# A four-stage transformer pipeline on one core: the wait for the rows of ones moved, and the last three layer norms shared with ScalarE

## The chip, the core and the metric

The kernel runs on one core of a Trainium2 chip. The core has a matrix engine (TensorE, PE in the profile, with its weight loads as PEld), a vector engine (VectorE, DVE), an engine for activation functions (ScalarE, ACT), a general engine (GpSimd, POOL) and a queue engine that issues the DMAs here (SyncE, SP). They run their own instruction streams and meet at semaphores. The metric is the device time of one execution in microseconds (us).

## The reference, cut to what matters

Input x has 8 batches of 512 tokens with 128 features. Four stages follow each other, each closed by a residual and a layer norm:

```python
x = layernorm(x + attention0(x))   # softmax attention, 16 heads of 8 features
x = layernorm(x + experts(x))      # 32 routed experts of width 64 (6 chosen per token), one shared of width 128
x = layernorm(x + attention1(x))   # RMS-normed q and k, rotary, sigmoid weights divided by their sum
x = layernorm(x + ffn(x))          # width 384: (silu(x Wg) * (x Wu)) Wd, weights int32 / 127
```

The layer norm of a row of 128 features is `(x - mean) / sqrt(var + 1e-5)`. The change touches the start of the first stage and the end of the last one.

## The kernel before, in words

**First attention.** q and k are split in three bf16 parts each; for each head the pairs of parts stand as 48 rows of a stack (`qs`, `ks`), two heads to a tile, one at partition 0 and one at 64. A first pass of scores (`s1`, L564) uses these 48 rows, and VectorE takes the maximum of every row of scores (`reduce_max`, L724). GpSimd splits the negated maxima in three parts (`split_max`, L788 to L794), TensorE turns them (`turn_max`, L542), ScalarE copies them out, and a DMA puts them under `qs` as rows 48 to 50. The second pass (`s2`, L629) multiplies 51 rows: rows 48 to 50 of `ks` are ones, so that the maximum is subtracted inside the product, and ScalarE takes the exponential (L483). The ones come from DRAM by DMA (`ones_rows`, L393, from `in_fill`), four of them, which raise `fill_in` to 64.

**The start.** Batch 0 takes a quicker way than the others. Its q and k products land in PSUM (L681), ScalarE and VectorE split them (L508 to L766), and for the first four heads (two stack tiles, `PLACED = 2`) TensorE puts the parts in place with products against a selection matrix (L695), which are copied to `qs` and `ks` (L516, L771; `placed`). The other heads go through DRAM: the SP queue writes the parts (L234, L240) and reads the stacks back (L253). Behind these reads stand, on the same queue, the ones for batch 0 (L393), the load of the residual X for all batches (L435), and the writes of batch 1's parts. Dummy products (`warm_up`, L533) stand between. GpSimd's first work on tensors is to split q and k of batch 1 (`split_qk`, L263 to L271); its stream waits for the load of X first (`pool.wait_ge(x_in, 16)`, ahead of `walk`). In the lead, which handles batch 0 alone, TensorE walks a fixed list of turns, two per unit: 56 scores, one V product, q and k of batch 1 (L554), and after the 39th score `turn_max` of the first half of the heads. Then `s2` begins. All orders here are written out by hand; there is no scheduler.

**The end.** The last stage (`last_stage`) has three hidden slices per batch, 24 units. Per unit TensorE makes gate and up products (L2220 to L2222), ScalarE silu (L2279), VectorE the product `hid` (L2309), ScalarE its rounded part `hh` (L2285), GpSimd the rest `hl` (L2352; VectorE for the last, L2335), and three units later TensorE adds the down products (L2244 to L2250). At the end of a batch ScalarE takes the sums (`take_down`, L2291), TensorE turns them (`turn`, L2257), VectorE adds X (L2318) and takes mean and variance (L149, L153), GpSimd makes `rstd` with an addition and a power (L183, L185), VectorE scales (L162, for the last batch L2326), and SP writes the batch out (L2209, and the last batch in two halves, L2213). Batches alternate between two banks (`out_bank`: 6 and 7), so a batch's first down product waits until the batch two before it has been scaled (`x_done`).

## Time and profile before

| | us |
|---|---|
| median of 3 runs | 1071.41 (1071.37 to 1071.44) |
| the profiled execution, its own time | 1071.79 |
| span of the profile | 1070.0 |
| PE busy | 1004.1 (94%) |
| DVE busy | 807.5 (75%) |
| ACT busy | 737.0 (69%) |
| POOL busy | 475.0 (44%) |

The span runs from the first instruction to the last event; the device time is 1.79 us longer in the profiled execution. Times in rows count from the start of the span. A row of the timeline merges equal instructions that follow each other; the duration is the time in which at least one of them was busy. Matmuls overlap: one of 512 columns is shown with 0.39 us, and the next can start 0.22 us after it at the full clock. PE counts as busy with dummy products too, so its 94% do not say that it is the limit.

### The profile page before, as it was taken

To read this page: it belongs to the slowest core of one execution; us is meant where nothing else is said; L and a number is where in the kernel's file an instruction comes from. 1 tells how busy PE (TensorE), PEld (TensorE's weight loads), DVE (VectorE), ACT (ScalarE), POOL (GpSimd) and SP (SyncE) were. 2 spreads that over 40 slices of the span, in tenths; PEclk is the share of its full clock that TensorE was granted. 3 is DMA by queue.
4 is the path that set the end of the run, shared out by engine and by line. 5 is a ranking of instruction groups with operands and counts; after the bars stand their busy time and mean duration, and the time that the engine had idled before them with its cause. 6 is when DMAs were issued, how large, how long until landed. Compare 5 with 4: busy or idle time off the path is not lost. (4 is left out here: it accounts for less than half of the span.)

```text
span 1070.0 us, 20246 instructions
## 1 busy us (share of the span) xinstructions
PE 1004.1 (94%) x5869; PEld 479.0 (45%) x5869; DVE 807.5 (75%) x1864; ACT 737.0 (69%) x955; POOL 475.0 (44%) x485
## 2 busy tenths in 40 slices
PE   4999999999999998999999999988999999999996
PEld 2322222222222235888888887762232323222485
DVE  3899999999999975897788789956456545632477
ACT  2047877777777786655555555557988898899754
POOL 0313414235143725676677677565332333220175
PEclk7999999999999999999999999999999999999999
DMA  6264122231221003234333432442512331230011
GB/s 194 93 223 125 46 86 75 70 114 45 86 81 52 2 2 115 93 114 149 113 93 123 140 111 80 145 145 68 161 63 65 118 112 58 65 118 1 1 31 50
DMA packets 73981, 96.98 MB, mean 91 GB/s; under 512 B 12668, under 2 KB 42236, under 8 KB 73532
## 3 DMA queue, kind: packets, MB, share of 16 engines
q1 hardware_dynamic: 73928, 96.33, 28.8%
q8 instruction: 26, 0.43, 0.2%
q14 instruction: 27, 0.22, 0.1%
HBM read 68.11 MB, written 27.79 MB: 90 GB/s over the span
## 5 line engine op out<-in xcount | busy, mean ns | idle before, releaser
L724 DVE TENSOR_REDUCE a_nmax<-a_ps_f 128x1 f32<-128x512 f32 x512 | 320.1, 683 | 28.2 <-PE a_ps_f L564 27.6
L483 ACT ACTIVATE a_prob<-a_ps_s 128x1024 f32<-128x1024 f32 x256 | 251.7, 1022 | 76.2 <-PE a_ps_s L629 74.9
L1314 ACT ACTIVATE a_prob<-a_ps_s 128x1024 f32<-128x1024 f32 x256 | 244.8, 1030 | 35.7 <-PE a_ps_s L1368 34.8
L2141 POOL TENSOR_TENSOR moe_hl<-moe_hid,moe_hh 128x512 fp32r<-128x512 f32 x135 | 175.2, 1303 | 90.1 <-ACT moe_hh L2026 90.0
L564 PE MATMUL a_ps_f<-a_ks,a_qs 48*128 48x512 bf16 x512 | 157.9, 387 | 22.2 <-DMA a_ks<-in_fill 10.7
L2016 ACT ACTIVATE moe_ps<-moe_ps 128x512 f32<-128x512 f32 x128 | 74.5, 582 | 112.0 <-PE moe_ps L1943 111.4
L1381 PE MATMUL a_ps_o<-a_prob,a_va 128*32 128x512 f32 x1024 | 137.3, 608 | 1.0 <-ACT a_prob L1314 0.5
L642 PE MATMUL a_ps_o<-a_prob,a_va 128*32 128x512 f32 x1024 | 136.4, 605 | 0.5 <-ACT a_prob L483 0.4
L629 PE MATMUL a_ps_s<-a_qs,a_ks 51*128 51x512 bf16 x512 | 132.5, 381 | 1.7 <-ACT a_prob L483 1.5
L564 PEld LDWEIGHTS a_ps_f<-a_ks,a_qs 48*128 48x128 bf16 x512 | 39.8, 93 | 202.6 <-DVE a_nmax L724 161.3
L2067 DVE TENSOR_TENSOR moe_prod<-moe_cw,moe_ps 128x512 f32<-128x512 f32 x128 | 87.3, 682 | 29.7 <-PE moe_ps L1943 29.1
L1368 PE MATMUL a_ps_s<-a_qs,a_ks 48*128 48x512 bf16 x512 | 92.7, 387 | 12.7 <-ACT a_prob L1314 9.4
L2076 DVE TENSOR_TENSOR moe_hid<-moe_prod,moe_ps 128x512 f32<-128x512 f32 x128 | 86.9, 679 | 6.6 <-DVE moe_prod L2067 1.9
L2026 ACT ACTIVATE moe_hh<-moe_hid 128x512 fp32r<-128x512 f32 x136 | 84.7, 624 | 3.7 <-DVE moe_hid L2076 3.6
L263 POOL TENSOR_TENSOR a_parts<-a_qk,g_zero 128x512 bf16<-128x512 f32 x28 | 29.2, 1044 | 126.1 <-ACT a_qk L455 65.7
L1368 PEld LDWEIGHTS a_ps_s<-a_qs,a_ks 48*128 48x128 bf16 x512 | 23.6, 93 | 134.2 <-ACT a_prob L1314 107.2
L788 POOL TENSOR_TENSOR a_msplit<-a_nmax,g_zero 128x32 bf16<-128x32 f32 x16 | 3.8, 239 | 145.6 <-DVE a_nmax L724 145.6
L1941 PE MATMUL moe_ps<-moe_xh,moe_whig 128*128 (+1 forms) x136 | 54.8, 403 | 2.0 <-DVE moe_hid L2076 2.0
L1966 PE MATMUL moe_ps<-moe_hl,moe_whid 128*128 128x512 f32 x136 | 53.9, 396 | 1.5 <-POOL moe_hl L2141 1.5
L1941 PE MATMUL moe_ps<-moe_xh,moe_whiu 128*128 (+1 forms) x136 | 53.8, 395 | 0.0
L1942 PE MATMUL moe_ps<-moe_xh,moe_wlog 128*128 (+1 forms) x136 | 53.7, 395 | 0.0
L1961 PE MATMUL moe_ps<-moe_hh,moe_wlod 128*128 128x512 f32 x136 | 53.7, 395 | 0.0
(304 smaller groups left out, 1630.6 us busy)
## 6 DMA issues: line engine op xcount, KB each, us to landing
moe_cw<-r_weights SPq DMA_DIRECT2D x256, 128.0 KB, 2.9
parts_q<-a_parts SPq DMA_DIRECT2D x48, 256.0 KB, 2.5
parts_k<-a_parts SPq DMA_DIRECT2D x48, 256.0 KB, 2.5
a_qs<-parts_q SPq DMA_DIRECT2D x126, 96.0 KB, 2.4
a_ks<-parts_k SPq DMA_DIRECT2D x126, 96.0 KB, 2.4
a_xt<-in_x_t SPq DMA_DIRECT2D x8, 256.0 KB, 3.0
out_x<-g_X SPq DMA_DIRECT2D x7, 256.0 KB, 2.3
moe_wg<-in_wg SPq DMA_DIRECT2D x1, 1088.0 KB, 6.7
```

The source lines that it names most:

```text
L483: nc.scalar.activation(prob[:, u % PSLOTS, :, :], ps_s[:, u % 2, :, :], ACT.Exp, scale=float(P) ** -0.5).then_inc(exp_done, 1)
L564: nc.tensor.matmul(ps_f[:, bank, :], stack_rows(qs[p], h, QKR)[:, qt * P:(qt + 1) * P], stack_rows(ks[p], h, QKR), start=True, stop=True). ...
L629: mm = nc.tensor.matmul(ps_s[:, u % 2, i, :], stack_rows(ks[p], h, MXR)[:, kt * P:(kt + 1) * P], stack_rows(qs[p], h, MXR), start=True, st ...
L642: mm = nc.tensor.matmul(ps_o[j * CT:(j + 1) * CT, :], v_of_head(va[p], kt, grp * HG + j), prob[:, (2 * e + j // UN) % PSLOTS, j % UN, :], ...
L724: nc.vector.tensor_reduce(nmax[:, half_no, h % 2, col:col + 1], ps_f[:, bank, :], AX.X, ALU.max, negate=True).then_inc(max_done, 1)
L1314: nc.scalar.activation(prob[:, u % PSLOTS, :, :], ps_s[:, u % 2, :, :], ACT.Sigmoid, scale=float(HD) ** -0.5).then_inc(exp_done, 1)
L1368: mm = nc.tensor.matmul(ps_s[:, u % 2, i, :], stack_rows(ks[p], h, QKR)[:, kt * P:(kt + 1) * P], stack_rows(qs[p], h, QKR), start=True, st ...
L1381: mm = nc.tensor.matmul(ps_o[j * CT:(j + 1) * CT, :], v_of_head(va[p], kt, grp * HG + j), prob[:, (2 * e + j // UN) % PSLOTS, j % UN, :], ...
L1941: nc.tensor.matmul(dst, w[0][:, j, :], hi, start=True, stop=False)
L2067: nc.vector.tensor_tensor(prod[:, bank(j), :], cw[:, slot(j), :], ps_u[:, bank(j), :], ALU.mult).then_inc(prod_done, 1)
L2076: nc.vector.tensor_tensor(hid[:, hid_at(j), :], prod[:, bank(j), :], ps_g[:, bank(j), :], ALU.mult).then_inc(hid_done, 1)
L2141: nc.gpsimd.tensor_tensor(hl[:, part_at(j), :], hid[:, hid_at(j), :], hh[:, part_at(j), :], ALU.subtract).then_inc(hl_done, 1)
```

## The change

At the start, the wait for the rows of ones (`fill_in`) stands ahead of the first `s2` of batch 0 instead of ahead of the whole walk. The selection products go tile by tile (both q and k of tile 0, then of tile 1), and their readers wait for other counts. The dummy products ahead of them are two instead of four. At the end, batches 5, 6 and the second half of 7 are scaled on ScalarE as `rstd * y + shift`, where `shift = -mean * rstd` comes from VectorE; batch 5's `rstd` still comes from GpSimd, those of 6 and 7 from a ScalarE root and a VectorE reciprocal. Batch 7's down sums go to bank 0 (a gate bank that is free then) and their transposes to the first halves of banks 0 and 1, so its first down product no longer waits for batch 5's scaling.

```diff
-WARM = (5, 4, 3)
+WARM = (5, 2, 3)
...
-                act.wait_ge(first_done, 4 + (1, 2, 4)[k])
+                act.wait_ge(first_done, 4 + (1, 3, 4)[k])
...
+                if is_first(b) and u == 0:
+                    pe.wait_ge(fill_in, 4 * 16)
                 if u in (0, NU // 2):
...
-            for n in range(2):
-                pe.wait_ge(first_mid, 2 * n + 2)
-                pe.wait_ge(first_low, 2 * n + 2)
-                for j in range(PLACED):
+            for j in range(PLACED):
+                for n in range(2):
+                    if j == 0:
+                        pe.wait_ge(first_mid, 2 * n + 2)
+                        pe.wait_ge(first_low, 2 * n + 2)
...
             pe.wait_ge(cleared, 5)
-            pe.wait_ge(fill_in, 4 * 16)
             walk(pe, units)
...
-            dve.wait_ge(first_done, 4 + 3)
+            dve.wait_ge(first_done, 4 + 2)
...
         def out_bank(b):
-            return ps[:, 6 + b % 2, :]
+            return ps[:, 6 + b % 2, :] if b < NB - 1 else ps[:, (N - NH3) % RG, :]
+
+        def tiles(b):
+            if b < NB - 1:
+                return out_bank(b).rearrange("p (k d) -> p k d", k=NT)
+            return ps[:, 0:2, 0:T // 2].rearrange("p n (k d) -> p n k d", k=NT // 2)
...
-            for i in range(2):
-                sp.wait_ge(ln["x_done"], NB + i)
+            for i, (done, value) in enumerate(((x_last, 1), (ln["x_done"], NB))):
+                sp.wait_ge(done, value)
...
-                elif j == 0 and b >= 2:
+                elif j == 0 and 2 <= b < NB - 1:
                     pe.wait_ge(ln["x_done"], b - 1)
...
+            def deviation(b):
+                n = LATE_B.index(b)
+                st, at = stats_of(b)
+                act.wait_ge(st["dve"], 2 * NT * (at + 1))
+                nc.scalar.activation(rs[:, n, :], st["mv"][:, :, 1], ACT.Sqrt,
+                                     bias=g["eps"][:, 0:1]).then_inc(std_done, 1)
+
+            def apply(b, which):
+                n = LATE_B.index(b)
+                act.wait_ge(shift_done, n + 1)
+                for k in which:
+                    y = tiles(b)[:, k, :] if b < NB - 1 else tiles(b)[:, k // 2, k % 2, :]
+                    ins = nc.scalar.activation(X[:, b, k, :], y, ACT.Identity, scale=scale_of(b)[:, k:k + 1],
+                                               bias=shift[:, n, k:k + 1])
+                ins.then_inc(ln["x_done"], 1)
...
+                if s == N:
+                    nc.scalar.activation(last.table[:, :], g["zero"][:, :], ACT.Sqrt)
+            apply(LATE_B[0], range(NT))
+            deviation(LATE_B[1])
+            apply(LATE_B[1], range(NT))
+            deviation(LATE_B[2])
+            apply(LATE_B[2], range(NT // 2, NT))
...
+                if b == NB - 1:
+                    scale(NB - 2)
                 dve.wait_ge(y_done, b + 1)
...
+            def scale(b):
+                n = LATE_B.index(b)
+                dve.wait_ge(std_done, n)
+                nc.vector.reciprocal(rs[:, n, :], rs[:, n, :]).then_inc(rs_done, 1)
+                dve.wait_ge(rs_done, n)
+                shifts(b)
...
             def apply_last():
                 b = NB - 1
-                dve.wait_ge(ln_last["pool"], 2)
-                for k in range(NT):
-                    ins = nc.vector.tensor_scalar(X[:, b, k, :], tiles(b)[:, k, :], ln_last["mv"][:, k, 0:1],
-                                                  ln_last["rstd"][:, k:k + 1], ALU.subtract, ALU.mult)
-                    if k % 2:
-                        ins.then_inc(ln["x_done"], 1)
+                for k in range(NT // 2):
+                    ins = nc.vector.tensor_scalar(X[:, b, k, :], tiles(b)[:, 0, k, :], ln_last["mv"][:, k, 0:1],
+                                                  rs[:, 2, k:k + 1], ALU.subtract, ALU.mult)
+                ins.then_inc(x_last, 1)
...
                 if s == N:
+                    dve.wait_ge(ln["pool"], 2 * (NB - 3) + 2)
+                    shifts(NB - 3)
                     dve.wait_ge(hh_done, N)
...
-                if batch_at(s, Y_AT) is not None:
-                    b = batch_at(s, Y_AT)
-                    layernorm_pool(nc, pool, g, *((ln, b) if b < NB - 1 else (ln_last, 0)))
+                if batch_at(s, Y_AT) is not None and batch_at(s, Y_AT) < NB - 2:
+                    layernorm_pool(nc, pool, g, ln, batch_at(s, Y_AT))
```

The order in which TensorE works at the start, before the change (`a_ps_s<-a_parts,a_prob` is a selection product, `a_ps_f<-a_ks,a_qs` a score of the first pass, `x5` counts equal rows):

```order
L695 MATMUL a_ps_s<-a_parts,a_prob 112x512 [waits a0_first_mid,a0_first_low,a0_first_rest,a0_select_in]
L695 MATMUL a_ps_s<-a_parts,a_prob 112x512 x5
L695 MATMUL a_ps_s<-a_parts,a_prob 112x512 [waits a0_first_low,a0_first_mid]
L695 MATMUL a_ps_s<-a_parts,a_prob 112x512 x5
L564 MATMUL a_ps_f<-a_ks_88,a_qs_87 128x512 [waits a0_placed0,a0_fill_in,a0_stack_in0,a0_cleared,consts_in]
```

And the same place in the changed kernel:

```order
L699 MATMUL a_ps_s<-a_parts,a_prob 112x512 [waits a0_first_mid,a0_first_low,a0_first_rest,a0_select_in]
L699 MATMUL a_ps_s<-a_parts,a_prob 112x512 x2
L699 MATMUL a_ps_s<-a_parts,a_prob 112x512 [waits a0_first_low,a0_first_mid]
L699 MATMUL a_ps_s<-a_parts,a_prob 112x512 x8
L565 MATMUL a_ps_f<-a_ks_88,a_qs_87 128x512 [waits a0_placed0,a0_stack_in0,a0_cleared,consts_in]
```

The score no longer waits for `a0_fill_in`, and the second half of the parts is needed three products earlier. The wait now stands on the first 51-row product (L632), behind 56 scores of the same stream.

ScalarE's stream at the very end, in the changed kernel (before it ended with the second `ff_dsb` row here, without the table load between):

```order
L2312 ACTIVATE ff_dsb<-ff_ps 128x512 [waits ff_t_done,ff_d_done]
L2306 ACTIVATE ff_hh<-ff_hid 128x512 [waits ff_d_done,ff_hid_done]
L2339 ACT_TABLE_LOAD
L2339 ACTIVATE a_table<-g_zero 128x1
L2312 ACTIVATE ff_dsb<-ff_ps 128x512 [waits ff_t_done,ff_d_done]
L2326 ACTIVATE g_X<-ff_ps,ff_shift,ff_rstd 128x128 [waits ff_shift_done]
L2326 ACTIVATE g_X<-ff_ps,ff_shift,ff_rstd 128x128 x3
L2318 ACTIVATE ff_rs<-ff_mv,g_eps 128x4 [waits ff_ln_dve]
L2326 ACTIVATE g_X<-ff_ps,ff_shift,ff_rs 128x128 [waits ff_shift_done]
L2326 ACTIVATE g_X<-ff_ps,ff_shift,ff_rs 128x128 x3
L2318 ACTIVATE ff_rs<-last_mv,g_eps 128x4 [waits last_ln_dve]
```

Behind these rows stand the two halves of batch 7 (`L2326`). Four scalings of batch 6 now stand between two roots on one engine. VectorE's stream at the end of the changed kernel:

```order
L2359 TENSOR_TENSOR ff_ps<-ff_ps,g_X 128x2x256 [waits ff_t_done]
L2368 RECIPROCAL ff_rs<-ff_rs 128x4 [waits ff_std_done]
L2374 SCALAR_TENSOR_TENSOR ff_shift<-ff_mv,ff_rs 128x4 [waits ff_rs_done]
L150 BN_STATS last_st<-ff_ps 128x6 [waits ff_y_done]
L150 BN_STATS last_st<-ff_ps 128x6 x3
L152 MEMSET last_gate 128x1 [waits last_ln_dve]
L154 BN_AGGR last_mv<-last_st 128x2 x4
L2368 RECIPROCAL ff_rs<-ff_rs 128x4 [waits ff_std_done]
L2374 SCALAR_TENSOR_TENSOR ff_shift<-last_mv,ff_rs 128x4 [waits ff_rs_done]
L2380 TENSOR_SCALAR g_X<-ff_ps,last_mv,ff_rs 128x128 x2
```

Before, four scalings of batch 6 stood behind `last_mv` and ahead of four of batch 7 (`g_X<-ff_ps,...`), and four of batch 5 stood between the last two `ff_hid`. Now VectorE scales two tiles in all here, and between the last addition and its statistics stands a reciprocal that waits for ScalarE's root.

## Rows read from the trace of the kernel before

**Rows 1.** Windows: stretch, length, PE, PEld, DVE, ACT, POOL busy, clock share, DMA share, GB/s
```profile
62.40:168.00 105.60, 101.41 (x658) 27.62 (x658) 100.46 (x184) 82.06 (x93) 35.48 (x49) 1.00 0.34 111
```
**Rows 2.** Timeline to 40 us: start, busy, engine, line, operation, count, idle before and releaser
```profile
9.99 2.77 PE L695 MATMUL a_ps_s<-a_parts,a_prob 128*112 128x512 bf16 x12 [0.31 <-issue]
...
20.58 0.88 SPq L435 DMA_DIRECT2D g_X<-in_x  x1
...
23.42 0.61 PE L564 MATMUL a_ps_f<-a_ks,a_qs 48*128 48x512 bf16 x2 [10.66 <-DMA a_ks<-in_fill]
...
29.11 0.39 PE L564 MATMUL a_ps_f<-a_ks,a_qs 48*128 48x512 bf16 x2
...
38.02 1.04 POOL L263 TENSOR_TENSOR a_parts<-a_qk,g_zero 128x512 bf16<-128x512 f32 x1 [37.11 <-ACT a_qk L455]
```
**Rows 3.** The load of X (L435), from issue to landing
```profile
DMA to landing us min/median/max: 11.1/11.1/11.1
```
**Rows 4.** Timeline of 40 to 63 us
```profile
41.48 1.15 POOL L271 TENSOR_TENSOR a_parts<-a_rest,a_parts 128x512 bf16<-128x512 f32 x1
...
43.90 1.04 POOL L263 TENSOR_TENSOR a_parts<-a_qk,g_zero 128x512 bf16<-128x512 f32 x1 [1.27 <-ACT a_qk L455]
...
49.44 0.24 POOL L794 TENSOR_TENSOR a_msplit<-a_mrest,a_msplit 128x32 bf16<-128x32 f32 x1
...
51.79 0.26 PE L542 MATMUL a_ps_f<-a_identb,a_msplit 128*96 128x128 bf16 x1 [0.21 <-DVE a_nmax L724]
...
58.88 0.51 PE L564 MATMUL a_ps_f<-a_ks,a_qs 48*128 48x512 bf16 x2
...
60.08 0.51 PE L564 MATMUL a_ps_f<-a_ks,a_qs 48*128 48x512 bf16 x2
...
62.47 0.39 PE L629 MATMUL a_ps_s<-a_qs,a_ks 51*128 51x512 bf16 x2
```
**Rows 5.** Windows of 1 us, columns as in rows 1
```profile
15.00:16.00 1.00, 0.00 (x0) 0.00 (x0) 0.00 (x0) 0.00 (x0) 0.00 (x0) 0.59 0.13 41
28.00:29.00 1.00, 1.00 (x3) 0.21 (x3) 0.97 (x2) 0.00 (x0) 0.00 (x0) 0.58 1.06 293
745.00:746.00 1.00, 1.00 (x8) 0.46 (x9) 0.96 (x4) 0.00 (x0) 0.00 (x0) 0.82 0.98 345
749.00:750.00 1.00, 1.00 (x10) 0.11 (x5) 0.00 (x0) 1.00 (x2) 0.00 (x0) 0.98 0.82 209
```
**Rows 6.** PE's timeline of 713 to 750 us, two idle stretches
```profile
719.25 0.61 PE L1368 MATMUL a_ps_s<-a_qs,a_ks 48*128 48x512 bf16 x4 [1.73 <-ACTq L1319]
...
744.93 0.66 PE L1351 MATMUL a_ps_f<-g_ident,a_xr 128*128 128x128 f32 x4 [1.51 <-DVE a_xr L1470]
```
**Rows 7.** Timeline of the last 14 us
```profile
1058.77 0.47 PE L2244 MATMUL ff_ps<-ff_hh,ff_whid 128*128 128x512 f32 x1 [0.36 <-DVE g_X L162]
...
1059.25 0.63 ACT L2285 ACTIVATE ff_hh<-ff_hid 128x512 fp32r<-128x512 f32 x1 [0.20 <-DVE ff_hid L2309]
...
1061.59 0.60 ACT L2291 ACTIVATE ff_dsb<-ff_ps 128x512 f32<-128x512 f32 x1 [1.71 <-PE ff_ps L2250]
...
1062.93 0.70 DVE L2318 TENSOR_TENSOR ff_ps<-ff_ps,g_X 128x512 f32<-128x512 f32 x1 [0.38 <-PE ff_ps L2257]
...
1064.69 0.28 DVE L153 BATCH_NORM_AGGREGATE last_mv<-last_st 128x2 f32<-128x6 f32 x3
...
1066.37 1.37 DVE L2326 TENSOR_SCALAR g_X<-ff_ps,last_mv,last_rstd 128x128 f32<-128x128 f32 x4
1067.13 1.01 SPq L2213 DMA_DIRECT2D out_x<-g_X  x2
```
**Rows 8.** ScalarE's timeline around a table load in the second stage
```profile
437.47 1.28 ACT L998 ACT_TABLE_LOAD   x1
438.76 0.28 ACT L998 ACTIVATE moe_exp<-moe_ps 128x128 f32<-128x128 f32 x1
```
**Rows 9.** Groups by form: line to count, then busy us, mean ns, idle before
```profile
L1795 DVE RECIPROCAL r_den<-r_den 128x4 f32<-128x4 f32 x8 | 1.4, 177 | 0.3
```

More of the change, by code:

```diff
@@ L142, in layernorm_buffers @@
             "rstd": sb("rstd", [P, NT]), "gate": sb("gate", [P, 1]),
-            "dve": sem("ln_dve"), "pool": sem("ln_pool"), "centred": sem("ln_centred"), "x_done": sem("x_done")}
+            **{k: sem(k if k == "x_done" else "ln_" + k) for k in signals}}
 def layernorm_stats(nc, dve, ln, b, y):
     for k in range(NT):
-        nc.vector.bn_stats(ln["st"][:, k, :], y[:, k, :]).then_inc(ln["dve"], 1)
+        tile = y[:, k, :] if len(y.shape) == 3 else y[:, k // 2, k % 2, :]
+        nc.vector.bn_stats(ln["st"][:, k, :], tile).then_inc(ln["dve"], 1)
     dve.wait_ge(ln["dve"], 2 * NT * b + NT)
@@ L2189, in last_stage, with scale_of, stats_of @@
                              "t_done", "y_done"))
-        last_lo, ln_last = sem("last_lo"), layernorm_buffers(ctx, nc, "last")
+        last_lo, ln_last = sem("last_lo"), layernorm_buffers(ctx, nc, "last", ("dve",))
+        LATE_B = (NB - 3, NB - 2, NB - 1)
+        rs, shift = sb("rs", [P, 3, NT]), sb("shift", [P, 3, NT])
+        std_done, rs_done, shift_done, x_last = sem("std_done"), sem("rs_done"), sem("shift_done"), sem("x_last")
         def out_bank(b):
-            return ps[:, 6 + b % 2, :]
+            return ps[:, 6 + b % 2, :] if b < NB - 1 else ps[:, (N - NH3) % RG, :]
[3 more added lines that the diff above has]
+            return ps[:, 0:2, 0:T // 2].rearrange("p n (k d) -> p n k d", k=NT // 2)
+        def scale_of(b):
+            return ln["rstd"] if b == LATE_B[0] else rs[:, LATE_B.index(b), :]
+        def stats_of(b):
+            return (ln, b) if b < NB - 1 else (ln_last, 0)
         def batch_at(s, at):
@@ L2256, in turn @@
                 for q in range(NT):
-                    mm = nc.tensor.transpose(out_bank(b)[:, q * P:(q + 1) * P], dsb[:, q * P:(q + 1) * P],
+                    to = tiles(b)[:, q, :] if b < NB - 1 else tiles(b)[:, q // 2, q % 2, :]
+                    mm = nc.tensor.transpose(to, dsb[:, q * P:(q + 1) * P],
                                              g["ident"][:, :])
@@ L2338, in _ @@
                     add_x(batch_at(s, Y_AT))
-                if batch_at(s, Y_AT) == NB - 1:
-                    layernorm_apply(nc, dve, g, ln, NB - 2, tiles(NB - 2))
-                elif batch_at(s, APPLY_AT) is not None and batch_at(s, APPLY_AT) < NB - 2:
+                if batch_at(s, APPLY_AT) is not None and batch_at(s, APPLY_AT) < NB - 3:
                     layernorm_apply(nc, dve, g, ln, batch_at(s, APPLY_AT), tiles(batch_at(s, APPLY_AT)))
                 elif batch_at(s, APPLY_AT) == NB - 1:
+                    scale(NB - 1)
                     apply_last()
```

17 lines of the change are left out of this document (10 added, 7 removed).

## The prediction

> **What bounds the kernel now.** I read the windows by stage, then the timeline of the start and of the end, then the clock. In the first attention's steady stretch VectorE is busy 100.46 of 105.60 us [rows 1]: it is the pace there, and a start that comes earlier should be kept as long as VectorE's first maximum comes earlier. It comes late: TensorE ends the selection products at 9.99 + 2.77 = 12.76 us, then stands idle 10.66 us until 23.42, released by the DMA that writes the ones [rows 2]. No first-pass score reads these rows. At the end nothing overlaps any more: after the last down product come ScalarE's copy (61.59), the transposes, VectorE's addition (62.93), statistics that end at 64.69 + 0.28 = 64.97, GpSimd's root until 66.37, four scalings in 1.37 us, and the last write [rows 7]. The reader is to see two separate gains, each with something that could come to stand in its place.
>
> **The wait for the ones.** Without it the first score waits only for its stacks, whose copies follow the selection products, and for these products themselves on TensorE. Their order by tile brings the first pair of copies earlier, but the second half of the parts is needed earlier too, and TensorE still has twelve of them to do: the first score starts at about 12.9. The reorder and the two dummy products fewer I cost at nothing (from −0.3 to +0.3 us): TensorE works on until 12.76 either way. So scores start 23.42 − 12.9 = 10.5 us earlier.
>
> The clock adds to it. The granted clock fell to half (1.2 instead of 2.4 GHz) at about 15.2 us, in that idle stretch (the mean share of 0.59 in that microsecond means 18% of it at full), and came back at about 28.8 [rows 5]. Meanwhile three pairs of scores took from 23.42 to 29.11, 5.69 us [rows 2]; at the full clock a pair takes 60.08 − 58.88 = 1.20 us [rows 4], three take 3.6. Without the idle stretch 2.1 us more are saved. TensorE would be at `turn_max` (L542), which stood at 51.79 [rows 4], at 51.79 − 10.5 − 2.1 = 39.2.
>
> But this instruction waits for GpSimd, and GpSimd's stream does not move with the scores. Its first split waits for the load of X, which stands on SP's queue behind the same transfers as before: issued at 20.58, landed 11.1 us later, at 31.7 [rows 2, 3]. Before, it was hidden: GpSimd started at 38.02, when ScalarE had q [rows 2]. Now q is there some 12.6 us earlier, at about 25.3, and X is last. From 31.85 (0.15 us from release to start) the split of q takes 41.48 + 1.15 − 38.02 = 4.61 us, and k and the split of the maxima 49.44 + 0.24 − 43.90 = 5.78 us [rows 2, 4]; the pause of 1.27 us between them goes, since k is there by then. GpSimd ends at 31.85 + 4.61 + 5.78 = 42.25 and `turn_max` starts at 42.4, 9.4 us earlier than before, not 12.6. From it to the first 51-row product (62.47) [rows 4] is 10.7 us of scores in VectorE's pace, as before; pairs of 1.20 us are its pace already, so nothing is caught up. Behind `turn_max` in TensorE's stream wait the last 16 scores, and VectorE for those. The moved wait itself costs nothing: the ones land by 23.4 and are asked for at 53.
>
> TensorE is idle from 39.2 to 42.4, 3.2 us. Does the clock fall? It fell about 2.4 us into the idle stretch at the start, and just after one of 1.51 us that ended at 744.93, but not for one of 1.73 us that ended at 719.25 [rows 5, 6]. I take that it falls. It then stays low for about 749.04 − 745.64 = 3.4 us (shares 0.82 and 0.98) [rows 5], or at worst the 5.4 us from 23.42 to 28.8. Of each low microsecond 1 − 1.20 / 1.90 = 0.37 is lost, so 1.3 us, at worst 2.0. The start brings 9.4 − 1.3 = 8.1 us; ends 7.2 and 9.7.
>
> The rest of the three attention and expert stages keeps its order. One thing moves with time: the low clock at 745.6 to 749.0 followed an idle stretch no longer than one that left the clock alone [rows 5, 6], so such falls can appear or vanish. Each is worth at most 3.4 × 0.37 = 1.3 us. I take zero and keep ±1.3.
>
> **The end.** The first down product of batch 7 waited 0.36 us for batch 5's scaling [rows 7]; this goes. Batch 5's four scalings leave VectorE ahead of its last hidden product, and the 0.20 us that ScalarE waited for it go too [rows 7]. I take 0.4 us for ScalarE's copy: 61.19 instead of 61.59. What is late next is the new table load, on ScalarE between the last `hh` (which would end at 59.25 − 0.20 + 0.63 = 59.68) and this copy. Loads took 1.28 us, with 0.02 us on either side [rows 8], and the small root behind it at most the 0.28 us of a 128x128 activation: 61.2, just covered; another 0.1 to 0.2 us would show.
>
> The Trainium skill (ScalarE: Activation LUTs, What ACT_TABLE_LOAD costs) says that every switch costs the load and a drain, about 2.66 us together. In rows 8 the next activation starts right behind the load, so this trace does not bear the drain out; by the rule the copy would start at about 62.5.
>
> Then ScalarE scales. This trace has no activation with a scale and a bias per partition. From below stands the 128x128 activation with 0.28 us [rows 8], four of them at most 1.1 us, and 0.8 us if they overlap by 0.1 us each (an estimate); from above the one of 512 columns with 0.60 us [rows 7], four 2.4 us. Nearest in kind is VectorE's scaling of the same tiles with the same two operands, four in 1.37 us [rows 7], and I take that.
>
> By the same page and section each such operand adds about 93 ns; an estimate from its figures is 1.6 us for four, which would leave about 0.6 us of the gain at the end instead of 0.9.
>
> Laid out: copy 61.19, VectorE's addition 62.53 to 63.23. ScalarE scales batch 5 from 61.7 to 63.1 and takes the root for batch 6 to 63.3. VectorE's reciprocal (0.18 us [rows 9]) waits for it and, with `shift`, lets the statistics of batch 7 start at 63.6, about as before: the 0.4 us is spent. They end at 64.9. ScalarE is scaling batch 6 from 63.75 to 65.12, so the root of batch 7 comes at 65.12 and ends at 65.35; reciprocal and `shift` until 65.7; VectorE scales two tiles until 66.43, ScalarE the other two until 66.54. GpSimd's way took from 64.97 to 66.37; the new one takes until 65.7, and half of the scalings are beside it. The last write is issued at about 66.9 (the first of the two holds the queue) instead of 67.74, the end of the four scalings [rows 7]. Gain 0.9 us. With 0.8 us for four it is 1.2; with 2.4 us the statistics start at 64.6, the root of batch 7 at 67.2, and it is a loss of 1.2 us.
>
> **The sum.** 8.1 + 0.9 = 9.0 us. The profiled execution took 1071.79 us, its span 1070.0 and 1.79 outside it; it would become 1062.8. It was 0.38 us above the median of 1071.41, against which the forecast is 1062.4.
>
> **The rivals.**
>
> *The clock holds.* If TensorE's idle stretch at `turn_max` does not lower the clock, as at 719.25, the start brings 9.4 us: 1071.41 − 10.3 = 1061.1. For it: the stretch could be cut if TensorE arrives later. Against: 3.2 us is longer than the 2.4 us after which it fell. A vanished fall at 745 would give a similar time.
>
> *GpSimd does not hold it.* Were X there before q, `turn_max` would move by the whole 12.6 us: 1071.41 − 12.6 − 0.9 = 1057.9. For it speaks only that a landing time is of one execution; the queue ahead of X is unchanged.
>
> *The gain at the start is given back.* If something not seen pins the first exponentials or the loop (such as the loads behind the stacks), only the end is left: 1070.5. Against: in the steady stretch VectorE idles 5 us in 106 [rows 1], and all else moves along.
>
> *Slower: the clock stays low through the lead.* With fewer dummy products and scores of only 48 rows, TensorE could be left at 1.2 GHz from its first scores. A pair then takes 1.90 us instead of 1.20, the 28 pairs 53 us, and the first 51-row product starts at 12.9 + 53 = 66 plus V, q and k (about 2 us), 68 instead of 62.47: 1071.4 + 5.6 − 0.9 = 1076. It decides from (9.4 + 0.9) / 0.70 = 15 pairs at the low clock on. Against: from 28.8 us on the same mix of scores and dummies ran at the full clock [rows 5].
>
> *The end is lost, by the drain.* If the switch of tables took twice what rows 8 show, the copy and all behind it would come 1.3 us later, for a loss of 0.4 us at the end: 1071.41 − 8.1 + 0.4 = 1063.7. For it speaks nothing in the trace; against it, that the activation at 438.76 follows the load at once [rows 8]. It is the case of the skill's drain, named above.
>
> **How the numbers follow.** Forecast (clock falls once, end near +0.9) 0.48; the drain 0.04; the clock holds, or a fall elsewhere vanishes, 0.32; GpSimd does not hold it 0.04; given back 0.06; slower 0.06. Likeliest time 1062.4. The range reaches down to the clock that holds with one fall less, 1061.1 − 1.3 = 1059.8, and up to the price of 2.0 us for the fall with an end worth nothing, 1071.41 − 7.4 = 1064.0, rounded to 1064.3. A measurement of this kernel can tell 0.2%, 2.1 us. Faster: the first four of these cases and half of the given-back one (its 1070.5 lies within 0.2%, but it may be given back in part), 0.91; within 0.2%: 0.03; slower 0.06.
>
> **What would show it.** In the new profile: first score at 12.9 (later would be the copies); GpSimd's first split at 31.8, not at q; an idle stretch of TensorE ahead of `turn_max` released by GpSimd's last split, near 42.4; clock share of 0.5 for about 3.4 us behind it; first exponential near 54.8; at the end ScalarE's last copy no longer idle for long before it, no `rstd` on GpSimd for batches 6 and 7, the root of batch 7 released by ScalarE's own scalings rather than by the statistics. I am wrong if the first split starts elsewhere, if the steady loop takes longer than before, or if the time from ScalarE's last copy of sums to the end of the span (1070.0 − 61.59 − 1000 = 8.4 us before) does not fall to about 7.9.

## The result and the profile after

The changed kernel took 1065.78 us (median of four executions, 1064.63 to 1067.31); the kernel before, beside it, 1071.43 us (1071.37 to 1073.59). The ratio is 0.9935, with a 95% interval from 0.9908 to 0.9962. The forecast was 1062.4 us with a range up to 1064.3: the direction was right, the time was not. Of a forecast gain of 9.0 us the profile shows 4.5 (span 1070.0 before, 1065.5 after); it is of the slowest of the four executions (1067.31), and by the medians 5.65 us were gained and 3.4 are missing. One execution of the kernel before in a later comparison took 4970.9 us and is left out of every figure.

At the start each row came where it was forecast. The timeline of the changed kernel to 55 us (columns as in rows 2):

```profile
9.81 3.08 PE L699 MATMUL a_ps_s<-a_parts,a_prob 128*112 128x512 bf16 x12 [0.76 <-DVE a_rest L765]
12.82 0.39 PE L565 MATMUL a_ps_f<-a_ks,a_qs 48*128 48x512 bf16 x2
...
31.69 1.04 POOL L264 TENSOR_TENSOR a_parts<-a_qk,g_zero 128x512 bf16<-128x512 f32 x1 [30.78 <-DMA g_X<-in_x]
...
41.80 0.24 POOL L797 TENSOR_TENSOR a_msplit<-a_mrest,a_msplit 128x32 bf16<-128x32 f32 x1
...
42.19 0.24 PE L543 MATMUL a_ps_f<-a_identb,a_msplit 128*96 128x128 bf16 x1 [2.80 <-POOL a_msplit L797]
...
54.65 1.02 ACT L484 ACTIVATE a_prob<-a_ps_s 128x1024 f32<-128x1024 f32 x1 [11.84 <-PE a_ps_s L632]
```

The first score starts at 12.82 us (12.9 forecast; 23.42 in [rows 2]). GpSimd's first split is released by the load of X at 31.69 (31.85 forecast; 38.02 in [rows 2], where ScalarE released it). TensorE waits 2.80 us for GpSimd's last split and is at `turn_max` at 42.19 (42.4 forecast; 51.79 in [rows 4]). The first exponential comes at 54.65, 8.25 us earlier than before.

The reader is to look for the rest in the clock column. Windows of the changed kernel, columns as in rows 1 (the ninth number of a row, ahead of the DMA share, is the clock share; 0.50 is 1.2 GHz):

```profile
42.30:45.60 3.30, 3.30 (x9) 0.77 (x9) 1.35 (x3) 0.27 (x1) 0.00 (x0) 0.50 0.59 197
...
406.00:407.00 1.00, 0.00 (x0) 0.00 (x0) 0.00 (x0) 0.49 (x1) 0.00 (x0) 1.00 0.60 191
407.50:410.90 3.40, 3.40 (x10) 2.87 (x11) 0.85 (x3) 2.07 (x3) 1.28 (x1) 0.50 0.60 166
411.00:412.00 1.00, 1.00 (x6) 0.81 (x5) 0.87 (x3) 0.16 (x1) 0.00 (x0) 1.00 0.85 207
...
670.40:673.70 3.30, 3.30 (x9) 2.61 (x8) 1.69 (x4) 1.63 (x3) 1.28 (x1) 0.50 0.21 75
...
714.70:718.10 3.40, 3.40 (x20) 2.06 (x20) 1.49 (x8) 2.40 (x3) 3.04 (x8) 0.50 0.57 177
...
742.00:745.40 3.40, 3.40 (x18) 0.48 (x20) 1.29 (x3) 1.88 (x2) 0.00 (x0) 0.50 0.52 161
```

The first of these was forecast, and the last answers to that of 745.6 to 749.0 in [rows 5]. The three between them are new. TensorE's timeline shows an idle stretch of more than a microsecond ahead of each (the number in brackets is the idle time). Those at 407 and 714 us stand at boundaries of stages, directly behind it. The one at 670 us stands inside the experts, 1.4 us behind the transposes of X for the second attention, which followed an idle stretch of 1.63 us:

```profile
407.50 1.09 PE L974 MATMUL moe_ps<-g_ident,moe_dsb 128*128 128x128 f32 x4 [1.74 <-PEq L296]
...
668.24 0.66 PE L1113 MATMUL moe_ps<-g_ident,g_X 128*128 128x128 f32 x4 [1.63 <-DVE a_turned L1080]
...
714.33 0.72 PE L1371 MATMUL a_ps_s<-a_qs,a_ks 48*128 48x512 bf16 x4 [1.72 <-ACTq L1322]
...
741.04 0.66 PE L1354 MATMUL a_ps_f<-g_ident,a_xr 128*128 128x128 f32 x4 [1.53 <-DVE a_xr L1473]
```

The third row is the stretch of [rows 6] that was 1.73 us long and left the clock alone in the kernel before.

To see what each costs, the same instruction was looked up in both traces, and its start before subtracted from its start after. This shift is −8.24 us up to the end of the first attention and changes only at the low stretches: to −6.6 behind 407 us, from −6.5 to −4.9 behind 670 us, to −3.9 behind 715 us, and not behind 742 us, since the kernel before has its own low stretch there. It is −3.80 us at the last stage. The steady stretch keeps its pace (VectorE busy 100.9 of 106.0 us in its window from 54 to 160 us, 100.46 of 105.60 in [rows 1]).

The end, in the timeline of the changed kernel (add 3.8 us to compare with rows 7):

```profile
1055.14 0.62 ACT L2306 ACTIVATE ff_hh<-ff_hid 128x512 fp32r<-128x512 f32 x1
...
1055.78 1.28 ACT L2339 ACT_TABLE_LOAD   x1
...
1057.08 0.20 ACT L2339 ACTIVATE a_table<-g_zero 128x1 f32<-128x1 f32 x1
...
1057.39 0.60 ACT L2312 ACTIVATE ff_dsb<-ff_ps 128x512 f32<-128x512 f32 x1
1057.88 1.50 ACT L2326 ACTIVATE g_X<-ff_ps,ff_shift,ff_rstd 128x128 f32<-128x128 f32 x4
...
1060.91 0.28 DVE L154 BATCH_NORM_AGGREGATE last_mv<-last_st 128x2 f32<-128x6 f32 x3
1061.39 0.30 ACT L2318 ACTIVATE ff_rs<-last_mv,g_eps 128x4 f32<-128x4 f32 x1
1061.73 0.18 DVE L2368 RECIPROCAL ff_rs<-ff_rs 128x4 f32<-128x4 f32 x1 [0.53 <-ACT ff_rs L2318]
...
1062.14 0.81 ACT L2326 ACTIVATE g_X<-ff_ps,ff_shift,ff_rs 128x128 f32<-128x128 f32 x2 [0.44 <-DVE ff_shift L2374]
...
1062.77 0.89 SPq L2233 DMA_DIRECT2D out_x<-g_X  x2
```

On the old scale (less 1000) ScalarE's copy comes at 1057.39 + 3.80 − 1000 = 61.19, as forecast; the statistics of batch 7 end at 1061.19 + 3.80 − 1000 = 64.99 (64.9 forecast), its root starts at 65.19 (65.12 forecast), and the last scalings end at 1062.95 + 3.80 − 1000 = 66.75 (66.54 forecast). The end brings 0.7 us instead of 0.9: 0.4 ahead of ScalarE's copy, as forecast, and 0.3 behind it. From that copy to the end of the span are 1065.5 − 1057.4 = 8.1 us, where the prediction named 7.9 as its sign.

### The profile page after: what moved, and what is told of

Read it like the earlier page. It is cut to its first block and busy times, and to the rows that moved or that the text cites. A ratio compares the mean times of both kernels' runs of the same rounds, so it can differ in the third digit from the quotient of the medians.

```text
span 1065.5 us, 20246 instructions
## 1 busy us (share of the span) xinstructions
PE 1008.0 (95%) x5867; PEld 481.8 (45%) x5867; DVE 805.6 (76%) x1859; ACT 742.8 (70%) x969; POOL 472.6 (44%) x481
## 5 line engine op out<-in xcount | busy, mean ns | idle before, releaser
L632 PE MATMUL a_ps_s<-a_qs,a_ks 51*128 51x512 bf16 x512 | 132.6, 381 | 1.7 <-ACT a_prob L484 1.5
L1371 PE MATMUL a_ps_s<-a_qs,a_ks 48*128 48x512 bf16 x512 | 92.9, 389 | 12.3 <-ACT a_prob L1317 9.0
```

The costliest lines, as they stand in the source:

```text
L632: mm = nc.tensor.matmul(ps_s[:, u % 2, i, :], stack_rows(ks[p], h, MXR)[:, kt * P:(kt + 1) * P], stack_rows(qs[p], h, MXR), start=True, st ...
L1371: mm = nc.tensor.matmul(ps_s[:, u % 2, i, :], stack_rows(ks[p], h, QKR)[:, kt * P:(kt + 1) * P], stack_rows(qs[p], h, QKR), start=True, st ...
```

## The experiments

Three readings of the 4.4 us that the profile lost between the start and the last stage were open. **A**: granted-clock falls at idle stretches of TensorE that may or may not fall in an execution. **B**: the new end or the new order of the selection products costs it. **C**: transfers or barriers at the boundaries give back part of any gain. Below, "shift" is always against the first profile of the kernel before. Each ratio is against the executions of the kernel before on the same chip beside it.

**Only the wait is moved.** The kernel before, with this edit alone:

```diff
             def s2(b, p, u):
+                if is_first(b) and u == 0:
+                    pe.wait_ge(fill_in, 4 * 16)
...
-            pe.wait_ge(fill_in, 4 * 16)
             walk(pe, units)
```

> The kernel before with one edit: the wait for the ones stands ahead of the first sums of probabilities (s2) instead of ahead of all scores. Order of the selection products, dummy products and the whole end are as before. Theory A (clock): the first exponential is 8.0 to 9.0 us earlier than before (GpSimd's split still starts at about 31.7 us), and this shift is kept on VectorE and ScalarE except where a low stretch of the clock stands in one kernel and not in the other; each such stretch takes 1.0 to 1.7 us of it. With two to four more stretches than before the time is 1071.4 - 8.3 + (2 to 5) = 1065 to 1068; the shift changes at low stretches and nowhere else. Theory B (the gain is lost in the new end or in the new order of the selection products): with neither of them in, the time is 1071.4 - 8.3 = 1063.1. Theory C (a fixed share of the gain is lost at the boundaries of stages, to transfers that do not come earlier): the shift shrinks at the two boundaries by more than the low stretches there explain, and TensorE waits there for a DMA.

Measured: 1065.94 us beside 1073.21 of the kernel before, ratio 0.9931 (0.9908 to 0.9955), which is the changed kernel's. The shift in its profile is −7.09 us at the first exponential, outside the 8 to 9 expected: the low stretch at `turn_max` was twice as long (41.9 to 48.6), and another stood at the start of the loop:

```profile
41.90:48.60 6.70, 6.51 (x17) 1.42 (x17) 3.27 (x5) 0.27 (x1) 0.05 (x1) 0.50 0.66 197
58.90:65.70 6.80, 6.45 (x28) 1.03 (x29) 3.97 (x7) 2.91 (x4) 3.24 (x5) 0.50 0.56 194
```

The second took 2.4 us of the shift, to −4.69, more than the 1.0 to 1.7 us expected of each. It is a place that the prediction did not think of. B falls for the start: with neither new order nor new end, the last stage comes 4.5 us earlier and not 8.3.

**Only the end is new.** The changed kernel with its start put back (the order of the selection products, too):

```diff
-WARM = (5, 2, 3)
+WARM = (5, 4, 3)
...
-                if is_first(b) and u == 0:
-                    pe.wait_ge(fill_in, 4 * 16)
...
+            pe.wait_ge(fill_in, 4 * 16)
             walk(pe, units)
```

> The changed kernel with its start (dummy products, order of the selection products, place of the wait for the ones) put back as before; only the end is new. Theory A: up to the last stage the instructions start when they did in the kernel before, to 0.2 us, the low stretches of the clock are those of before (one at about 15 to 29 us, one at about 746 to 749 us), and the time is 0.7 us less, 1070.7 (1070.2 to 1071.2). Theory B (the end costs what is missing): 1071.4 + 3 or more. The table load stands alone in 1.3 us and the next activation follows it at once; four scalings take 1.5 us.

Measured: 1071.48 us, ratio 0.9982 (0.9965 to 0.9999). In its profile the shift goes from +0.21 us at the last stage's hidden products to −0.41 where the last `rstd` is ready and −0.46 at the end of the span, so the end gives 0.7 us there; the ratio allows that and more. The time lies above the 1070.2 to 1071.2 expected. B falls for the end too. That it would start as the first profile of the kernel before, with the same low stretches, was wrong: the first stretch was 10.2 us long instead of 13.7, so that the first exponential came 1.5 us earlier, and it had one at 675 and one of 6.8 us at 719 us, and none at 746.

**GpSimd waits for X where it first reads it.** In the changed kernel:

```diff
                 if u0 == 0 and is_first(b):
+                    pool.wait_ge(x_in, 16)
                     front.split_weight(pool, 0)
...
-            pool.wait_ge(x_in, 16)
...
```

> The changed kernel with GpSimd's wait for X put where GpSimd first reads X (the first unit of batch 0) instead of ahead of its first split. Theory A: GpSimd's first split starts when ScalarE has q, at about 25.5 us instead of 31.7, the first maximum's transpose (turn_max) is no longer waited for by TensorE and comes at 39.2 to 39.8 us instead of 42.2, the low stretch of 3.4 us behind it is gone, and the first exponential comes 12 to 12.6 us earlier than in the kernel before (4 us earlier than in the changed one). The end follows, minus low stretches at the boundaries (0 to 3 of them at 1.0 to 1.7 us): 1071.4 - 12.3 - 0.7 = 1058.4 with none, up to 1063 with three. Rival (something behind the split holds the first maximum as well, such as VectorE's or GpSimd's later work on X): turn_max stays at about 42 and the time at 1065.8.

Measured: 1059.83 us (1058.54 to 1063.51), ratio 0.9876 (0.9849 to 0.9903). Its timeline, and two of its windows:

```profile
25.79 1.04 POOL L264 TENSOR_TENSOR a_parts<-a_qk,g_zero 128x512 bf16<-128x512 f32 x1 [24.87 <-ACT a_qk L456]
...
39.55 0.26 PE L543 MATMUL a_ps_f<-a_identb,a_msplit 128*96 128x128 bf16 x1 [0.21 <-DVE a_nmax L727]
...
50.66 1.95 ACT L484 ACTIVATE a_prob<-a_ps_s 128x1024 f32<-128x1024 f32 x2 [10.48 <-PE a_ps_s L632]
```

```profile
30.00:50.00 20.00, 19.74 (x82) 6.20 (x80) 18.63 (x32) 0.87 (x2) 5.71 (x9) 1.00 0.50 156
...
404.00:407.30 3.30, 3.30 (x10) 2.65 (x9) 1.30 (x4) 1.60 (x3) 1.28 (x1) 0.50 0.59 170
```

The split starts at q, `turn_max` is no longer held, the clock stays at 1.00, and the first exponential comes 12.24 us earlier than before. So the wait for X held the start, as the prediction said, and it cost 4.0 us against the changed kernel's first profile: 2.6 at `turn_max` (39.55 for 42.19), and 1.35 for the low stretch behind it. The shift stays at −12.23 until the one fall at 404 us, which takes 1.59.

**TensorE kept busy in the wait.** The changed kernel, with dummy products where it waits for GpSimd:

```diff
+HOLD = 12
...
+                        if is_first(b):
+                            warm_up(HOLD)
                         turn_max(b, 0)
```

> The changed kernel with twelve dummy products on TensorE directly ahead of the first maximum's transpose, where it otherwise waits 2.8 us for GpSimd. They take about 2.6 us at the full clock. Theory A: the clock stays high there, the transpose comes at the same 42.2 us, and the first exponential comes 1.2 us earlier than in the changed kernel (53.4 instead of 54.65). What the end of the program keeps of it depends on the low stretches at the boundaries: 1064.5 if they are the same as in the changed kernel, and 1.0 to 1.7 us more or less for each that comes or goes. Rival (the low stretch at 42.3 us does not come from the wait ahead of it): it stands there as before, and the time is unchanged or 0.1 us more.

Measured: 1066.05 us, ratio 0.9918 (0.9893 to 0.9942). The dummies did what they were for, and it brought nothing in this profile:

```profile
38.00:55.00 17.00, 16.55 (x73) 5.50 (x72) 13.98 (x24) 2.10 (x3) 3.28 (x7) 1.00 0.66 215
56.10:66.30 10.20, 9.85 (x42) 1.61 (x41) 6.62 (x11) 5.14 (x6) 4.74 (x5) 0.50 0.69 255
```

The first exponential came 9.73 us earlier, but a low stretch of 10.2 us at the start of the loop took 3.5 us of it (shift −6.20 behind it). That the fall is gone behind `turn_max` is shown; why another came at 56 us is not. TensorE had idled no longer than 0.21 us at a time from 38 us on. This is one profile.

**Both kernels again, twice.** The same two programs, unchanged.

> The changed kernel once more, unchanged. Theory A (which idle stretches lower the clock differs between executions of one program): the start and the steady stretches are as in the first profile to 0.2 us (turn_max at 42.2 us), but the low stretches behind the boundaries at 407, 670, 715 and 742 us are not all the same ones or not of the same length; the times spread over 2 us or more, and those with a lower mean granted clock are longer by about 0.4 us for each low microsecond. Rival (the four falls belong to the program): the same four stretches stand there, and the times agree to 0.5 us.

Measured: 1064.75 us (1063.95 to 1065.41), ratio 0.9923 (0.9906 to 0.994). Its profile has low stretches at 41 (6.8 us), 669 and 713 us and none at 407 or 742, so the falls differ between executions of one program, as expected. The other two parts were not borne out: the times spread over 1.5 us and not over 2 or more, and they do not follow the mean granted clock (1064.55 us at 0.989, 1065.41 at 0.991).

> The kernel before once more, unchanged. Theory A: at the boundaries (about 412, 675, 720 us) low stretches can stand that its first profile does not have, which gives times up to 6 us above the fastest; its median is above the 1071.4 of its first three runs. Rival: one fall at 746 us as in the first profile, and 1071.4 to 0.3 us.

Measured: 1072.01 us (1070.61 to 1073.29), ratio 0.9991 (0.998 to 1.0002). The median is above 1071.4, as expected. Three windows of its profile, two where the first profile has the clock at full and one where it has it low:

```profile
65.00:71.80 6.80, 6.45 (x27) 0.95 (x29) 3.90 (x7) 2.92 (x4) 3.32 (x5) 0.50 0.86 329
...
720.40:727.10 6.70, 6.26 (x26) 2.73 (x27) 3.82 (x14) 3.88 (x4) 4.17 (x9) 0.50 0.29 92
745.00:750.00 5.00, 3.48 (x28) 1.32 (x24) 2.77 (x7) 3.10 (x4) 2.09 (x2) 1.00 0.46 157
```

The fall at 746 us is not there, and two others are.

> The changed kernel, one more profiled execution. Theory A: turn_max at 42.2 us and a low stretch behind it; low stretches at some of the places seen so far (about 56, 407, 670, 714, 742 us) and at no others, not the same set as in both earlier profiles. Rival: the set of its first profile.

Measured: one execution, 1064.13 us. Its low stretches are at 43, 668 and 712 us; in its window from 404 to 408 us, over the first boundary, the clock share is 1.00.

> The kernel before, one more profiled execution. Theory A: one low stretch from about 15 to 17 us until 26 to 29 us, then a set out of about 65, 412, 675, 720 and 746 us; the end is later than the fastest execution by about 0.4 us for each low microsecond. Rival: one fall at 746 us alone, as in the first profile.

Measured: one execution, 1072.53 us, with low stretches at 16, 675 and 746 us.

**The boundaries filled.** In the changed kernel:

```diff
             pv(NB - 1, 1, NE - 1)
+            columns = identb[:, :].unsqueeze(1).broadcast_to([P, NT, P])
+            for _ in range(5):
+                nc.tensor.matmul(ps_s[:, 0, 0, :], identb[:, :], columns, start=True, stop=True)
...
+            def fill(b, count):
+                if routed and isinstance(b, int) and b == NB - 1:
+                    for _ in range(count):
+                        nc.tensor.matmul(ps_g[:, 0, 0:P], g["ident"][:, :], g["ident"][:, :], start=True, stop=True)
...
             def turn(b):
+                fill(b, 4)
                 pe.wait_ge(d_taken, b + 1 + C)
...
                 mm.then_inc(t_done, 1)
+                fill(b, 8)
```

> The changed kernel with dummy products on TensorE in three idle stretches at the boundaries: five behind the last product of the first attention (the idle stretch of 1.7 us ahead of the experts' first transposes), four and eight small ones around the last transposes of the experts (0.7 and 1.7 us). The idle stretch of 1.6 us ahead of the transposes of X for the second attention is left as it is. Theory A: no low stretch behind 407 and 715 us any more, that at 670 us may stand; the first exponential stays at 54.6 us, and the end keeps 1.6 to 3.5 us more of the gain than the first profile did: 1063.3 (1062 to 1065). Rival (the 4.4 us lost on the way are not the clock's): the time stays at 1065.8 or grows by the dummy products' 1 to 2 us, with the shift shrinking at the same places.

Measured: 1064.44 us (1063.62 to 1066.14), ratio 0.9921 (0.9902 to 0.994), the changed kernel's in its second comparison. Windows of its profile:

```profile
403.00:409.00 6.00, 4.58 (x30) 1.70 (x31) 0.28 (x1) 4.46 (x6) 0.00 (x0) 1.00 0.38 131
669.00:672.40 3.40, 3.40 (x10) 2.63 (x9) 1.90 (x5) 1.64 (x4) 1.28 (x1) 0.50 0.25 81
705.00:716.00 11.00, 9.37 (x59) 7.16 (x58) 3.47 (x13) 5.43 (x9) 5.58 (x7) 1.00 0.12 37
```

As expected, the two filled places are at full clock and the one left unfilled is low. One profile does not show that the fill did it: at the first boundary the clock fell in 2 of the 10 profiles without dummies there and in none of the 4 with them, at the second in 8 of 11 and in none of 3. And the gain is small: the eight dummies behind the transposes take 1.0 us by themselves, as the next kernel shows.

**Both causes taken out.** The late wait for X and the filled boundaries; then with three instead of eight products behind the transposes; then with the first boundary alone.

> GpSimd's wait for X put where it first reads X, and the dummy products of the boundaries as well: both causes taken out at once. Theory A: the first exponential comes 12.2 us earlier than in the kernel before, one low stretch at most on the way, and the times are 1057 to 1059 with less spread than without the dummy products (1058.5 to 1063.5). Rival: as without them, a median of 1059.8, or more by what the dummy products add at the boundaries.

Measured: 1059.81 us (1058.51 to 1062.05), ratio 0.9878 (0.9857 to 0.9899). The median is above the 1057 to 1059 expected. The shift is −12.2 us up to 700 us, with no low stretch, and −11.2 behind the boundary, again with none. VectorE waits 1.57 us for TensorE at the barrier there, in its timeline, where it waited 0.61 us in the changed kernel:

```profile
714.02 0.87 DVE L150 BATCH_NORM_STATS2 moe_st<-moe_y 128x6 f32<-128x128 f32 x4 [0.61 <-PEq L1811]
```

```profile
707.71 0.87 DVE L150 BATCH_NORM_STATS2 moe_st<-moe_y 128x6 f32<-128x128 f32 x4 [1.57 <-PEq L1814]
708.02 0.61 PE L1374 MATMUL a_ps_s<-a_qs,a_ks 48*128 48x512 bf16 x4 [0.90 <-ACTq L1325]
```

> GpSimd's wait for X at its first reader and the dummy products of the boundaries, but only three instead of eight behind the last transposes of the experts. With eight, the barrier ahead of the second attention waited for TensorE and the shift fell from 12.20 to 11.23 us there with no low stretch at the place. Theory A: the barrier waits for VectorE again as in the kernel before, the 1.0 us is back (first score of the second attention 12.2 us earlier than before), and the time is 1.0 us less: a median of 1058.8 (1057.4 to 1060.5). Rival: the low stretch behind 715 us comes back in most executions and the median stays at 1059.8.

Measured: 1059.95 us (1059.07 to 1060.52), ratio 0.9879 (0.9844 to 0.9915). With three the 1.0 us is back, in the profile (first product of the second attention at 707.11):

```profile
707.11 0.61 PE L1374 MATMUL a_ps_s<-a_qs,a_ks 48*128 48x512 bf16 x4 [1.05 <-ACTq L1325]
```

```profile
20.00:700.00 680.00, 660.50 (x3659) 340.41 (x3658) 600.00 (x1329) 442.90 (x607) 345.53 (x349) 1.00 0.31 100
733.90:737.20 3.30, 3.30 (x16) 0.34 (x12) 1.15 (x2) 1.86 (x2) 0.00 (x0) 0.50 0.41 126
```

So a clock share of 1.00 over 680 us is possible with all this work in it. Theory A holds for the profile (1059.07 us, the fastest of the four), and not for the median: that of four executions is still not below that without dummies, as the rival had it.

> GpSimd's wait for X at its first reader and only the five dummy products behind the last product of the first attention. Theory A: never a low stretch at 404 us (five executions with all dummies and none there), those at 666 and 706 us in some of the executions: 1057.5 to 1062, a median of 1059.3. Rival (the dummy products themselves delay the experts): the shift falls at 404 us by 0.3 us or more without a low stretch.

Measured: 1060.48 us (1058.62 to 1060.93), ratio 0.9884 (0.9849 to 0.9919). The median lies above the 1059.3 expected. Only profiled executions show where a low stretch stands, so the expectation rests on two profiles with a fill at 404 us and not on five executions; with this kernel and the one before it, four have none there. This profile has none at 404 us, no shift lost there, and one of 6.8 us at 706 us.

The medians of the late wait for X alone (1059.83 us) and of the three filled versions can't be told apart. All four beat both kernels.

## Why the prediction was wrong

The shift against the kernel before's first profile, read at the first exponential and then behind each place (times on the old scale), and the low stretches ahead of the last stage, as the trace's clock record has them (start, length in us):

| kernel, profile | 63 | 90 | 430 | 700 | 735 | 904 | span | low stretches |
|---|---|---|---|---|---|---|---|---|
| before, first | 0 | 0 | 0 | 0 | 0 | 0 | 1070.0 | 15 (13.7), 746 (3.4) |
| before, again | −1.1 | +1.4 | +1.4 | +1.6 | +2.9 | +1.5 | 1071.5 | 17 (10.2), 65 (6.8), 720 (6.8) |
| before, third | −1.6 | −1.0 | −1.0 | +0.5 | +0.5 | +0.6 | 1070.7 | 16 (10.2), 675 (3.4), 746 (3.4) |
| end only | −1.5 | −1.5 | −1.5 | +0.2 | +1.5 | +0.1 | 1069.5 | 16 (10.2), 675 (3.4), 719 (6.8) |
| after, first | −8.3 | −8.3 | −6.6 | −4.9 | −3.9 | −3.8 | 1065.5 | 42, 407, 670, 715, 742 (3.4 each) |
| after, again | −7.7 | −7.7 | −7.7 | −5.9 | −4.5 | −5.9 | 1063.4 | 41 (6.8), 669 (3.4), 713 (3.4) |
| after, third | −8.6 | −8.6 | −8.6 | −6.9 | −5.6 | −7.0 | 1062.3 | 43 (3.4), 668 (3.4), 712 (6.8) |
| wait only | −7.1 | −4.7 | −4.7 | −4.4 | −3.1 | −4.5 | 1065.5 | 42, 59, 714 (6.8 each) |
| dummies in the wait | −9.7 | −6.2 | −6.2 | −4.5 | −3.1 | −4.6 | 1064.8 | 56 (10.2), 670 (3.4), 715 (3.4) |
| boundaries filled | −7.7 | −7.7 | −7.7 | −6.0 | −5.0 | −5.0 | 1064.3 | 41 (6.8), 669 (3.4), 741 (3.4) |
| X late | −12.2 | −12.2 | −10.6 | −10.5 | −10.5 | −11.9 | 1057.4 | 404 (3.4) |
| X late, filled | −12.4 | −12.4 | −12.4 | −12.2 | −11.2 | −11.1 | 1058.2 | 735 (3.4) |
| X late, filled less | −12.4 | −12.4 | −12.3 | −12.1 | −12.1 | −12.0 | 1057.3 | 734 (3.4) |
| X late, first filled | −12.5 | −12.5 | −12.5 | −12.3 | −11.0 | −12.5 | 1056.8 | 706 (6.8) |

Along each row the shift changes by 0.25 us or less where no low stretch differs from the first row's, and by 1.0 to 3.5 us where one does. There are two exceptions: the 1.0 us of the eight dummies, and 0.65 us between 63 and 90 us in the third profile of the kernel before. There TensorE waited for the load of x, which it did not do in the first profile; its timeline:

```profile
78.50 1.12 PE L554 MATMUL a_ps_f<-a_xt,a_w 128*128 128x512 f32 x2 [0.59 <-DMA a_xt<-in_x_t]
```

**The failed step** is the sentence "Each is worth at most 3.4 × 0.37 = 1.3 us. I take zero and keep ±1.3." It treats falls elsewhere as one event of one known price. Nor does the range hold even that one: its upper end, 1064.0 rounded to 1064.3, takes the worst price at `turn_max` and an end worth nothing, and no fall elsewhere at all; with 1.3 us for one it would have been 1065.6, still short of 1065.78. The runs show four things in its place. The falls are several: at the start of the loop, at the boundary to the experts (407 us), ahead of their end (670), at the start of the second attention (714) and in its first batch (742) the clock fell in some profiles and not in others, of the same program too. The price is not at most 1.3 us for 3.4 us: a fall near 670 us took 1.6 us in each of the three profiles of the changed kernel, at 407 us 1.6, at 713 to 715 us 1.0 and 1.3, in the first batch of the second attention 1.5. They can be longer: at the start of the loop 6.8 and 10.2 us took 2.4 and 3.5 us. And the reference had its own: in its first profile, and so in what the forecast started from, only one fall stood behind the start, with its other two profiles 0.7 and 1.5 us longer. From the forecast's own steps the changed kernel's three profiles come out at −8.3, −7.7 and −8.6 us at the start (8.1 forecast), and the way from there to the last stage takes 4.5, 1.7 and 1.6 us (zero forecast). In the first profile 1.6 + 1.6 + 1.0 = 4.2 us of the 4.5 stand at its three new low stretches. In the executions without a profile the places of the falls are not known.

**How much of it is the clock.** The 56 executions of the kernel before that have a granted clock on record, 1069.69 to 1078.26 us, give the price without any trace: the two executions with a mean granted clock of 0.993 took 1069.89 us on average, the four with 0.984 took 1077.27. Since the low level is half the full one, 0.009 less is 0.018 × 1072 = 19.3 us more at the low level, and 7.4 / 19.3 = 0.38 us for each; a straight line through all 56 gives 0.38 too. The five executions with both causes taken out agree: from 1058.51 us at 0.999 to 1062.05 at 0.995 are 3.5 us for 0.008 × 1060 = 8.5 low ones, 0.42 each. As a mean the 0.37 of the prediction, from two rows of scores, was right, though single falls took up to 1.6 / 3.4 = 0.47; the number of low microseconds was not. The changed kernel's 11 executions (1063.95 to 1067.31) do not show this relation: their clocks differ by 0.005 at most, and at 714 us a fall of 6.8 us took little more than one of 3.4. That falls cost it time is shown by its three profiles, and for its other eight executions only argued.

**The wait for the ones, GpSimd and X**: right in the mechanism, and to 0.2 us for the first score, the first split and `turn_max`. The experiment with the wait for X gives 12.24 us for a start that is not held, where the rival had 12.6. **The fall behind `turn_max`**: it came in all five profiles with the wait and in none of the five where the wait was filled or gone; it took 1.2 and 1.3 us where it lasted 3.4 us (forecast 1.3) and 2.4 to 2.6 where it lasted 6.8, up to 0.6 above the worst that the prediction gave. **The selection products**: nothing, as costed. **The clock at the start**: the 2.1 us counted for the low stretch from 15 to 29 us was 1.6, since the scores behind it came 12.2 us earlier and the first one 10.6. The first three pairs take 16.82 − 12.82 = 4.0 us at the full clock, where the prediction put the 3.6 of the steady pace. GpSimd's wait for X hid this error. The two later profiles of the kernel before have 10.2 us there and 1.1 and 1.6 us less to give: that 8.3 us at the first exponential meets the 8.1 forecast is in part the luck of the reference, for against those two profiles it is 7.2 and 6.6.

**The end**: 0.7 us for 0.9, in all ten profiles with the new end. The terms that were mis-sized are four scalings on ScalarE, 1.50 us and not 1.37, and the last root, 0.30 us and not 0.23; both stand in the last chain. The table load was covered, as forecast. The Trainium skill (ScalarE: Activation LUTs, What ACT_TABLE_LOAD costs) gave 1.6 us by an estimate from its price of pointer operands, nearer than the 1.37 from the row of VectorE that I took. Its drain did not show: the load ended at 1055.78 + 1.28 = 1057.06 and the next activation started at 1057.08.

**The rivals**: the clock held at `turn_max` in none of the five profiles with the wait, and GpSimd held the start in all five. Slower and the end lost by the drain did not happen. Half of the gain was given back in the first profile, but by falls of the clock and not by something that pins the start. Theory C is out: kernels without a fall at a boundary lose nothing there, and the gain of the late wait for X passes all of them. With what is known now a better range would have been 1061 to 1067: 1062.4 less the 1.5 us of the fall at 746 us, and plus the 4.2 of three more.

**Open**: why a given idle stretch lowers the clock in one execution and not in the next, and whether the earlier start makes falls likelier at 407 and 670 us. Near 670 us all five profiles whose shift there was 6.0 to 8.5 us had one, and the four with 10.5 to 12.4 us none, nor the wait-only one with 4.5; but of the three of the kernel before and the end-only one, two had it as well. This is too few to tell.

## What to carry to other kernels

When a wait of TensorE is removed, the falls of its clock are part of the sum: list every stretch in which it idles for a microsecond or more (here the start of the real loop as well), and count each as an event that may come or not, with its own price, in the kernel before as well. Take the reference from several profiled executions, since a single one shows one draw of them; comparing instruction by instruction, the shift changes only where something happens (a fall, or once a load that came late), and that separates a mechanism that works from a gain lost later. And look for the next wait behind the one removed: here GpSimd's wait for a load that it did not yet read was worth 5 to 6 us more (a median of 1059.8 against 1064.8 and 1065.8), beside the 6 to 8 that the change brought.

## What the runs showed of the hardware

The granted clock was low for 3.4, 6.8, 10.2 or 13.7 us in these profiles, at the same place for different lengths in different executions of one program (41 to 43 us: 6.8 and 3.4). A stretch of 1.72 to 1.74 us without TensorE lowered it in some executions and not in others. It also fell, for 6.8 and 10.2 us, where TensorE had not been idle longer than 0.21 us at a time for 10 us before (at 56, 59 and 65 us, in three kernels). The price is not always in proportion: in the first microseconds of the second attention 3.4 us took 1.0 to 1.3 us and 6.8 us no more than 1.4, which fits TensorE catching up, though no run tested it.
